# A feed-forward layer on one Trainium2 core: two x tiles are loaded later, and the order of the work on the second pair of hidden tiles is changed

## Chip, core and metric

The kernel runs on one core of one Trainium2 chip. The metric is the device time of one execution in microseconds (us). Time and profile are those of the kernel before the change, unless something else is said.

## What is computed

The input x is eight sequences of 1024 tokens by 512 channels. Cut to what matters:

```python
def cond(y, zX, zY, zR):                # a five-point stencil over tokens and channels
    lap_x = left - 2*y + right          # neighbours by reflection at the borders
    lap_y = up - 2*y + down
    return zX*lap_x + zY*lap_y + zR*y*(1 - y)

def ffn(x, W1, b1, W2, b2, scale):      # W1 is 2048 x 512, W2 is 512 x 2048
    even, odd = x[:, 1:17:2], x[:, 2:17:2]
    m1 = outer(even[:, :4], odd[:, :4])     # 2048 x 512 of rank one pieces, per sequence
    m2 = outer(even[:, 4:], odd[:, 4:])     # 512 x 2048
    h = gelu(x @ (W1 + scale*m1).T + b1)
    return h @ (W2 + scale*m2).T + b2

out = x + ffn(cond(x, zX, zY, zR), W1, b1, W2, b2, scale)
```

## The kernel before

**Work of TensorE.** All is kept transposed: y, the result of the stencil, has 128 partitions by 4 channel groups by the tokens. A sequence is 8 tiles of y (x tile n has 128 tokens with a border), two halves of 512 tokens. Layer one makes 16 hidden tiles of 128 per half in PSUM (`ph`), in 8 pairs i; layer two adds each of them into four PSUM banks `po`. Each operand is split in two fp32r parts, a high one (`yh`, `W1h`, `gh`, `W2h`: a rounded copy made by ScalarE) and a low one (`yl`, `W1l`, `gl`, `W2l`: the difference, made by VectorE), and each product is three matmuls, high by high, low by high, high by low (L629, L631, L633 for layer one in `product`, L645 to L647 for layer two in `layer2`). From sequence 1 on layer one uses Strassen's scheme. The weights W1 and W2 of each pair get the rank one piece of their sequence first: for W1, ScalarE writes `scale * outer` into a buffer (`outer`, L840), and GpSimd starts a DMA that adds W1 from HBM onto it (`add_W1`: L519 for pair 1 of sequence 0, L521 for all others); for W2, VectorE adds the piece (`fold`, L1302), whose row comes as a broadcast load.

**The first 30 us.** The change is almost all here, in sequence 0. Nothing of y exists at the start, so the first pair and the first tiles are made in ways of their own:

- PE runs 18 warm-up matmuls (L672), then makes the neighbour sums of y tile 0 (`raw0`) and tile 1 (`sums1`, from sums `st` and `sd` that VectorE forms) as matmuls by diagonals, and rows for the outer products (`even_row`).
- y tiles 0 to 3 are finished by VectorE. For tiles 0 and 1: `mul(0, n)` (L1257), then `tile0(n)` (L1219), which adds the PSUM result. For tiles 2 and 3: the two neighbour sums `sd` = up + down and `st` = left + right (for tile 2 by VectorE in `sums0(2)`, L1202 and L1203; for tile 3 by GpSimd in `sums3`, L512 and L513), then `mul`, `fin` (L1262), `tile` (L1268).
- `pair0(n)` (L610) makes hidden pair 0 from plain fp32, tile by tile of y; it waits for `s_tile`.
- Pair 1 (L639) follows as three groups of 8 matmuls: `W1h` by `yh0`, `W1l` by `yh0`, `W1h` by `yl0`. `W1h` of pair 1 is made by `w1h_plain(1)` on ScalarE (L854), which waits for `d_raw1`, the landing of L519's DMA; `W1l` by `w1l_plain(1)` on VectorE (L1252); `yh0` and `yl0` by `part0_h` (L818) and `part0_l` (L1234).
- Layer two for the first hidden tile (L700) comes next: 4 matmuls each of `gh` by `W2h`, `gl` by `W2h`, `gh` by `W2l`. `W2h` comes from `w2h(0, 0)` (L883), this from `fold(0, 0)`, and this waits for a broadcast load of rows (L361, SyncE), which itself waits until the rows were stored to HBM (L359). Then the steady order of L645 to L647 and L629 to L633 begins.

**What sets the order.** All orders are written out by hand: each engine has a list of calls, in-order, with semaphores between them. SyncE's list is that of one DMA queue (q1 in the profile), GpSimd's DMAs are another (q0), ScalarE starts the loads of x tiles 0, 2 and 3 (q10). SyncE first issues x tile 1, W1 and W2 parts, `xn`, and x tiles 4 to 7 (L244), and only then the store of the rows.

The waits that matter here are few:

```python
e.wait_ge(s_mt, 1)       # sums3: GpSimd after VectorE's second sum of tile 2
e.wait_ge(s_outer, summed(b, i))   # add_W1
e.wait_ge(d_raw1, 16)    # w1h_plain(1)
e.wait_ge(d_row2, 16)    # SyncE, between L359 and L361
```

Of the kernel before, what the change touches and what calls it, by code (L numbers as in the profile page):

```python
# [5 lines left out]
def adaln_ffn_kernel(nc: bass.Bass, xT, xs, x, xn, pk, w1, w2, b2, out):  # L6
# [3 lines left out]
    ALU = mybir.AluOpType  # L10
# [10 lines left out]
    with ctx:  # L21
# [17 lines left out]
        yh0 = sb("yh0", [128, 5, 2, 512], f32r)  # L39
        yl0 = sb("yl0", [128, 5, 2, 512], f32r)  # L40
# [194 lines left out]
        def _(e):  # L235
# [7 lines left out]
            def load_x0(n):  # L243
                e.dma_start(Xs[n].rearrange("p r s -> p (r s)"), xT[0, n]).then_inc(d_x[n], 16)  # L244
# [110 lines left out]
            e.dma_start(xr[:, 0:2, :].rearrange("p a q -> p (a q)"), xn).then_inc(d_N, 16)  # L355
            for n in (4, 5, 6, 7):
                load_x0(n)
            e.wait_ge(s_flat, 1)
# [16 lines left out]
            load_W2(0, 7)  # L375
            load_EB1(0, 5)
            load_W2(0, 8)
            keep_W1(4)
            load_W2(0, 9)
            load_EB1(0, 6)  # L380
            load_W2(0, 10)
            load_W2(0, 11)
# [119 lines left out]
        def _(e):  # L502
            def diagonal(a, v):
                return e.affine_select(DG[:, a, :], v.broadcast_to([128, 128]), [[-1, 128]],
                                       ALU.is_equal, 0.0, base=0, channel_multiplier=1)

            def sums3():
                mid, up, down, left, right = x_at(0, 3)
                st, sd = sums_at(0, 3)
                e.wait_ge(d_x[3], 16)  # L510
                e.wait_ge(s_mt, 1)
                e.tensor_tensor(sd, up, down, ALU.add).then_inc(s_md, 1)  # L512
                e.tensor_tensor(st, left, right, ALU.add).then_inc(s_mt, 1)  # L513
# [36 lines left out]
            diagonal(1, zt[:, 0, 1:2]).then_inc(s_dg, 1)  # L550
            diagonal(0, zt[:, 0, 0:1]).then_inc(s_dg, 1)
            sums3()
            for i in range(1, NI):
# [25 lines left out]
        def _(e):  # L579
# [104 lines left out]
            for bank, lt, rows in ((ph[1], 0, 2), (ph[3], 1, 3)):  # L684
                e.wait_ge(s_outer, rows)
                for s in range(2):
                    term(bank, W1h, 2 * s + lt, yh0, s, s == 0, False)
            e.wait_ge(s_w1lB, 1)
            for bank, lt in ((ph[3], 1), (ph[1], 0)):
                for s in range(2):  # L690
                    term(bank, W1l, 2 * s + lt, yh0, s, False, False)
            e.wait_ge(s_ylt, 4)
            for bank, lt, done in ((ph[3], 1, s_plain), (ph[1], 0, s_p3)):
                for s in range(2):
                    mm = term(bank, W1h, 2 * s + lt, yl0, s, False, s == 1)
                mm.then_inc(done, 1)
# [85 lines left out]
        def _(e):  # L782
# [189 lines left out]
            e.wait_ge(d_N, 16)  # L972
            e.activation(nW, nM[:, 128:384], ACT.Identity, bias=zc[:, 1, 8:9], scale=zc[:, 0, 8:9]).then_inc(s_nw, 1)
            w1h_plain(2)
            scaled(0, 4)
            w2h(0, 0)
            w2h(0, 1)

# [174 lines left out]
        def _(e):  # L1153
# [37 lines left out]
            def sums1():  # L1191
# [4 lines left out]
                e.tensor_tensor(sd, up, down, ALU.add).then_inc(s_sd1, 1)  # L1196

            def sums0(n):
                mid, up, down, left, right = x_at(0, n)
                st, sd = sums_at(0, n)  # L1200
                e.wait_ge(d_x[n], 16)
                e.tensor_tensor(sd, up, down, ALU.add).then_inc(s_md, 1)  # L1202
                e.tensor_tensor(st, left, right, ALU.add).then_inc(s_mt, 1)  # L1203
# [166 lines left out]
            mul(0, 0)  # L1370
            sums0(2)
            tile0(0)
            fold0()
            mul(0, 1)
            tile0(1)
# [7 lines left out]
            part0_l(1)  # L1383
            w1l_plain(1)
            part0_l(2)
            part0_l(3)
            glE(0, 0, 0)
            fold(0, 0, 0, 4)
# [286 lines left out]
```

## Time and profile before

| what | value |
|---|---|
| median of 3 runs | 1335.42 us (1335.19 to 1335.44) |
| the profiled execution's own time | 1335.85 us |
| its span | 1334.6 us |
| PE busy | 1330.2 us (100%), 5896 instructions |
| PE weight loads | 1099.5 us (82%) |
| VectorE, ScalarE, GpSimd busy | 1034.8, 793.3, 255.9 us |
| granted TensorE clock | 1.0 throughout |

The span is from the first to the last instruction. Matmuls overlap in the profile (each is shown with 389 ns, though the next one starts 227 ns later), so PE's busy share says only that no long gap is there; the starts of the rows tell the rest. The page's sections 2 and 4 show the same: every slice of PE is at 9 tenths or more, and the chain of work that ended last is PE for 98% of the span.

### The profile page before, as it was taken

The page shows a single profiled execution, that of the slowest core. Times are in us where ns is not written, and L with a number is a line of the kernel's source. Part 1 is how long each engine was busy: PE and PEld are TensorE (multiplying, and loading weights), DVE is VectorE, ACT ScalarE, POOL GpSimd, SP SyncE. Part 2 cuts the span into 40 slices and gives each one's busy share as a digit, 9 for nine tenths or more (in the row PEclk, how much of TensorE's full clock was granted, in tenths as well). Part 3 has the DMA queues.
Part 4 walks back from the last instruction along what each step waited for, and adds up shares of the span by engine and source line. Part 5 has one row for each costly group of instructions (what it writes and reads, how often), then busy time and mean ns, then how long its engine had stood idle before and what let it go on. Part 6 is the DMA issues. An engine that isn't in the chain of part 4 may idle for free.

```text
span 1334.6 us, 17111 instructions
## 1 busy us (share of the span) xinstructions
PE 1330.2 (100%) x5896; PEld 1099.5 (82%) x5896; DVE 1034.8 (78%) x1774; ACT 793.3 (59%) x1372; POOL 255.9 (19%) x257
## 2 busy tenths in 40 slices
PE   9999999999999999999999999999999999999999
PEld 7888888888888888888888888888888888888887
DVE  8977799858897688976899668996689967665343
ACT  6644566645675556754677546675467754666432
POOL 1000122301232012320132201331022310232000
PEclk9999999999999999999999999999999999999999
DMA  8764377777778577876768667686767866676661
GB/s 253 195 155 151 83 203 212 205 213 207 189 202 201 183 214 197 212 188 203 205 189 222 179 219 192 194 218 173 231 176 210 210 188 201 162 191 164 173 195 50
DMA packets 140224, 253.79 MB, mean 190 GB/s; under 512 B 13669, under 2 KB 37481, under 8 KB 140137
## 3 DMA queue, kind: packets, MB, share of 16 engines
q1 hardware_dynamic: 122184, 201.69, 47.1%
q0 software_dynamic: 17520, 49.81, 22.3%
q10 hardware_dynamic: 432, 1.20, 0.2%
q8 instruction: 46, 0.75, 0.2%
q14 instruction: 42, 0.34, 0.1%
HBM read 189.61 MB, written 63.05 MB: 189 GB/s over the span
## 4 chain that ended last, share of the span: by engine, by line
PE 98%; DMA 1%; ACT 1%; DVE 0%; issue 0%; SPq 0%; ACTq 0%; DVEq 0%
PE po L645 17%; PE po L646 17%; PE po L647 17%; PE ph L629 15%; PE ph L631 15%; PE ph L633 15%; DMA R<-in_w_dram 1%; DMA x<-in_xT_dram 0%; PE po L700 0%; DVE xr L1366 0%; ACT DE L944 0%; ACT y L793 0%; ACT R L840 0%; ACT UVs L840 0%; ACT W1h L854 0%
## 5 line engine op out<-in xcount | busy, mean ns | idle before, releaser
L645 PE MATMUL po<-W2h,gh 128*128 128x512 f32 x1020 | 397.1, 389 | 0.0
L647 PE MATMUL po<-W2h,gl 128*128 128x512 f32 x1020 | 397.1, 389 | 0.0
L646 PE MATMUL po<-W2l,gh 128*128 128x512 f32 x1020 | 397.0, 389 | 0.0
L629 PE MATMUL ph<-yh,W1h 128*128 128x512 f32 x896 | 348.8, 389 | 0.0
L633 PE MATMUL ph<-yh,W1l 128*128 128x512 f32 x896 | 348.8, 389 | 0.0
L631 PE MATMUL ph<-yl,W1h 128*128 128x512 f32 x896 | 348.7, 389 | 0.0
L647 PEld LDWEIGHTS po<-W2h,gl 128*128 128x128 f32 x1020 | 191.5, 188 | 39.8
L645 PEld LDWEIGHTS po<-W2h,gh 128*128 128x128 f32 x1020 | 191.5, 188 | 39.8 <-DVE W2l L1310 0.2
L646 PEld LDWEIGHTS po<-W2l,gh 128*128 128x128 f32 x1020 | 191.5, 188 | 39.6
L629 PEld LDWEIGHTS ph<-yh,W1h 128*128 128x128 f32 x896 | 168.2, 188 | 35.1 <-issue 0.2
L633 PEld LDWEIGHTS ph<-yh,W1l 128*128 128x128 f32 x896 | 168.2, 188 | 35.0
L631 PEld LDWEIGHTS ph<-yl,W1h 128*128 128x128 f32 x896 | 168.2, 188 | 34.7
L1354 DVE TENSOR_TENSOR gl<-ph,gh 128x512 fp32r<-128x512 f32 x128 | 87.8, 686 | 112.8 <-ACT gh L926 112.6
L530 POOL TENSOR_TENSOR Ts<-R 128x512 f32<-128x512 f32 x56 | 75.4, 1346 | 445.5 <-DVE W1l L1321 390.4
L1359 DVE TENSOR_TENSOR gl<-ph,gh 128x512 fp32r<-128x512 f32 x128 | 87.3, 682 | 79.7 <-ACT gh L933 79.5
L1302 DVE SCALAR_TENSOR_TENSOR W2s<-EB,SC,W2s 128x128 f32<-128x128 f32 x480 | 142.3, 346 | 3.3 <-DMA W2s<-in_w_dram 2.3
L919 ACT ACTIVATE ph<-ph,PK 128x512 f32<-128x512 f32 x128 | 84.0, 656 | 75.8 <-DVE ph L1350 71.9
L1310 DVE TENSOR_TENSOR W2l<-W2s,W2h 128x512 fp32r<-128x512 f32 x124 | 112.2, 905 | 4.3 <-ACT W2h L883 4.2
L883 ACT ACTIVATE W2h<-W2s 128x512 fp32r<-128x512 f32 x124 | 77.9, 629 | 61.7 <-DVE W2s L1302 61.1
L926 ACT ACTIVATE gh<-ph 128x512 fp32r<-128x512 f32 x128 | 76.7, 599 | 63.1 <-PE po L647 59.0
L840 ACT ACTIVATE R<-EB,SC 128x256 f32<-128x256 f32 x240 | 101.8, 497 | 0.3 <-DMA EB<-ep_scratch 0.3
L909 ACT ACTIVATE ph<-ph,PK 128x512 f32<-128x512 f32 x128 | 83.7, 654 | 29.4 <-DVE ph L1344 16.0
(125 smaller groups left out, 1365.4 us busy)
## 6 DMA issues: line engine op xcount, KB each, us to landing
W2s<-in_w_dram SPq DMA_DIRECT2D x124, 256.0 KB, 3.8
R<-in_w_dram POOLq DMA_DIRECT2D x62, 512.0 KB, 7.1
uv_scratch<-UVs SPq DMA_DIRECT2D x112, 256.0 KB, 4.4
UVs<-uv_scratch SPq DMA_DIRECT2D x112, 256.0 KB, 3.9
X<-in_xT_dram SPq DMA_DIRECT2D x56, 390.0 KB, 4.8
xr<-in_x_dram SPq DMA_DIRECT2D x16, 1024.0 KB, 5.5
xr<-in_b_dram POOLq DMA_DIRECT2D x16, 1024.0 KB, 10.6
out_dram<-xr SPq DMA_DIRECT2D x64, 256.0 KB, 2.3
```

Of the source, the lines that this page charges most:

```text
L629: e.matmul(bank[:, :], W1h[:, f, blk, wc], yh[:, q, c, :], start=first and c == 0, stop=False, skip_group_check=not first)
L631: e.matmul(bank[:, :], W1h[:, f, blk, wc], yl[:, q, c, :], start=False, stop=False, skip_group_check=not first)
L633: mm = e.matmul(bank[:, :], W1l[:, f, blk, wc], yh[:, q, c, :], start=False, stop=c == 1, skip_group_check=not first)
L645: e.matmul(po[t][:, :], gh[:, lt, st], W2h[:, k, :], start=i == 0 and lt == 0, stop=False)
L646: e.matmul(po[t][:, :], gh[:, lt, st], W2l[:, k, :], start=False, stop=False)
L647: return e.matmul(po[t][:, :], gl[:, lt, st], W2h[:, k, :], start=False, stop=i == NI - 1 and lt == 1)
L840: m = e.activation(to[:, 2 * h:2 * h + 2, 128 * c:128 * c + 128], row.rearrange("p (a q) -> p a q", a=2), ACT.Copy, scale=SC[:, b % 2, cd, ...
L919: e.activation(bank[:, :], bank[:, :], ACT.Gelu, bias=b1t[:, k:k + 1]).then_inc(s_actL, 1)
L1302: m = e.scalar_tensor_tensor(w, rows2(b, n // 4)[:, a, :], SC[:, b % 2, ck, 4 + a:5 + a], w, ALU.mult, ALU.add)
L1310: e.tensor_tensor(W2l[:, k, :], w2s_at(b, n), W2h[:, k, :].bitcast(f32), ALU.subtract).then_inc(s_w2l, 1)
L1354: e.tensor_tensor(gl[:, 0, :], bank_of(b, h, i, 0)[:, :], gh[:, 0, :].bitcast(f32), ALU.subtract).then_inc(s_glE, 1)
L1359: e.tensor_tensor(gl[:, 1, :], bank_of(b, h, i, 1)[:, :], gh[:, 1, :].bitcast(f32), ALU.subtract).then_inc(s_glL, 1)
```

## The change

Four things are done, all in the first 60 us:

1. SyncE issues the loads of x tiles 6 and 7 no longer at the start, but after the loads `load_EB1(0, 5)` and `load_EB1(0, 6)`.
2. Of tile 2's two neighbour sums VectorE keeps up + down (`side2`) and GpSimd takes left + right (`token2`), ahead of its two sums of tile 3, which no longer wait for `s_mt`. VectorE's `mul(0, 1)` moves ahead of `side2`, `tile0(0)` and `fold0`.
3. PE takes `W1h` by `yl0` of pair 1 ahead of `W1l` by `yh0`; VectorE accordingly makes the low part of y tiles 2 and 3 ahead of `W1l`.
4. ScalarE takes `w2h(0, 0)` ahead of `w1h_plain(2)` and `w2h(0, 1)` ahead of `scaled(0, 4)`.

```diff
@@ block.sync
-            for n in (4, 5, 6, 7):
-                load_x0(n)
+            load_x0(4)
+            load_x0(5)
             e.wait_ge(s_flat, 1)
             e.dma_start(R2, rows[:, :]).then_inc(d_row2, 16)
             e.wait_ge(d_row2, 16)
...
             load_EB1(0, 5)
+            load_x0(6)
             load_W2(0, 8)
             keep_W1(4)
             load_W2(0, 9)
             load_EB1(0, 6)
+            load_x0(7)
@@ block.gpsimd
+            def token2():
+                mid, up, down, left, right = x_at(0, 2)
+                e.wait_ge(d_x[2], 16)
+                e.wait_ge(s_md, 1)
+                e.tensor_tensor(sums_at(0, 2)[0], left, right, ALU.add).then_inc(s_mt, 1)
...
                 e.wait_ge(d_x[3], 16)
-                e.wait_ge(s_mt, 1)
                 e.tensor_tensor(sd, up, down, ALU.add).then_inc(s_md, 1)
                 e.tensor_tensor(st, left, right, ALU.add).then_inc(s_mt, 1)
...
+            token2()
             sums3()
@@ block.tensor
-            e.wait_ge(s_w1lB, 1)
+            e.wait_ge(s_ylt, 4)
             for bank, lt in ((ph[3], 1), (ph[1], 0)):
                 for s in range(2):
-                    term(bank, W1l, 2 * s + lt, yh0, s, False, False)
-            e.wait_ge(s_ylt, 4)
+                    term(bank, W1h, 2 * s + lt, yl0, s, False, False)
+            e.wait_ge(s_w1lB, 1)
             for bank, lt, done in ((ph[3], 1, s_plain), (ph[1], 0, s_p3)):
                 for s in range(2):
-                    mm = term(bank, W1h, 2 * s + lt, yl0, s, False, s == 1)
+                    mm = term(bank, W1l, 2 * s + lt, yh0, s, False, s == 1)
@@ block.scalar
+            w2h(0, 0)
             w1h_plain(2)
+            w2h(0, 1)
             scaled(0, 4)
-            w2h(0, 0)
-            w2h(0, 1)
@@ block.vector
+            def side2():
+                mid, up, down, left, right = x_at(0, 2)
+                e.wait_ge(d_x[2], 16)
+                e.tensor_tensor(sums_at(0, 2)[1], up, down, ALU.add).then_inc(s_md, 1)
...
             mul(0, 0)
-            sums0(2)
+            mul(0, 1)
+            side2()
             tile0(0)
             fold0()
-            mul(0, 1)
             tile0(1)
...
             part0_l(1)
-            w1l_plain(1)
             part0_l(2)
             part0_l(3)
+            w1l_plain(1)
             glE(0, 0, 0)
```

On VectorE, from the sums of tile 1 to the last tile of y, this stood in a row before (the numbers L are lines of the kernel; `s` is the buffer of neighbour sums):

```order
L1195 TENSOR_TENSOR s<-x 128x512
L1196 TENSOR_TENSOR s<-x 128x512
L1257 TENSOR_TENSOR y<-y,x 128x4x128
L1202 TENSOR_TENSOR s<-x 128x512
L1203 TENSOR_TENSOR s<-x 128x512
L1219 TENSOR_TENSOR y<-y,po 128x4x128
L1228 SCALAR_TENSOR_TENSOR UVs<-ph,SC,UVs 128x2x128 x4
L1257 TENSOR_TENSOR y<-y,x 128x4x128
L1219 TENSOR_TENSOR y<-y,po 128x4x128
L1257 TENSOR_TENSOR y<-y,x 128x4x128
L1262 SCALAR_TENSOR_TENSOR y<-s,PK,y 128x4x128
L1268 SCALAR_TENSOR_TENSOR y<-s,PK,y 128x4x128
```

and this stands there now:

```order
L1203 TENSOR_TENSOR s<-x 128x512
L1204 TENSOR_TENSOR s<-x 128x512
L1270 TENSOR_TENSOR y<-y,x 128x4x128 x2
L1209 TENSOR_TENSOR s<-x 128x512
L1232 TENSOR_TENSOR y<-y,po 128x4x128
L1241 SCALAR_TENSOR_TENSOR UVs<-ph,SC,UVs 128x2x128 x4
L1232 TENSOR_TENSOR y<-y,po 128x4x128
L1270 TENSOR_TENSOR y<-y,x 128x4x128
L1275 SCALAR_TENSOR_TENSOR y<-s,PK,y 128x4x128
L1281 SCALAR_TENSOR_TENSOR y<-s,PK,y 128x4x128
```

One sum of tile 2 is gone, and the multiplication of tile 1 stands beside that of tile 0, so that behind `fold0` (L1228, now L1241) only the addition of tile 1 is left before tile 2 is worked on.

On GpSimd, between the diagonals and the DMAs that add W1, before:

```order
L504 AFFINE_SELECT DG<-ON 128x128
L504 AFFINE_SELECT DG<-PK 128x128 x2
L512 TENSOR_TENSOR s<-x 128x512
L513 TENSOR_TENSOR s<-x 128x512
L519 DMA UVs<-in_w_dram 128x1024
L521 DMA R<-in_w_dram 128x1024 x6
```

and now:

```order
L506 AFFINE_SELECT DG<-ON 128x128
L506 AFFINE_SELECT DG<-PK 128x128 x2
L513 TENSOR_TENSOR s<-x 128x512
L519 TENSOR_TENSOR s<-x 128x512
L520 TENSOR_TENSOR s<-x 128x512
L526 DMA UVs<-in_w_dram 128x1024
L528 DMA R<-in_w_dram 128x1024 x6
```

Three sums stand ahead of the DMA of W1's pair 1 where two stood.

On SyncE, from the start of its list to the second load of x, as a difference:

```order
 L271 DMA W2s<-in_w_dram 128x512 x2
 L355 DMA xr<-in_xn_dram 128x1024
-L244 DMA x<-in_xT_dram 128x780 x4
+L244 DMA x<-in_xT_dram 128x780 x2
 L359 DMA row_scratch<-rows 4x128
 L361 DMA EB<-row_scratch 128x512
```

The store of the rows and their broadcast load stand behind two x tiles instead of four.

## Rows read from the trace of the kernel before

**Rows 1.** Timeline of PE: start us, duration us, engine, line, operation, count, and idle time before.

```profile
0.85 3.87 PE L672 MATMUL ph<-const-bfloat16-1.0 128*128 128x256 bf16 x18 [0.85 <-PEq L1665]
...
12.00 7.50 PE L610 MATMUL ph<-y,UVs 128*128 128x128 f32 x64
19.26 2.07 PE L639 MATMUL ph<-yh,W1h 128*128 128x512 f32 x8
...
22.99 1.98 PE L639 MATMUL ph<-yl,W1h 128*128 128x512 f32 x8
25.22 1.19 PE L700 MATMUL po<-W2h,gh 128*128 128x512 f32 x4 [0.26 <-ACT W2h L883]
...
28.07 0.39 PE L645 MATMUL po<-W2h,gh 128*128 128x512 f32 x1
...
1330.89 0.39 PE L647 MATMUL po<-W2h,gl 128*128 128x512 f32 x1
```

**Rows 2.** One stretch, busy us by engine: PE, PEld, DVE, ACT, POOL; clock, DMA share, GB/s.

```profile
17.00:17.50 0.50, 0.50 (x6) 0.38 (x4) 0.50 (x2) 0.07 (x1) 0.00 (x0) 1.00 1.11 197
```

**Rows 3.** Timeline of VectorE.

```profile
11.36 0.90 DVE L1257 TENSOR_TENSOR y<-y,x 128x512 f32<-128x512 f32 x1
12.36 0.69 DVE L1219 TENSOR_TENSOR y<-y,po 128x512 f32<-128x512 f32 x1
...
16.65 0.75 DVE L1268 SCALAR_TENSOR_TENSOR y<-s,PK,y 128x512 f32<-128x512 f32 x1
...
23.05 1.14 DVE L1302 SCALAR_TENSOR_TENSOR W2s<-EB,SC,W2s 128x128 f32<-128x128 f32 x4 [0.98 <-DMA EB<-row_scratch]
...
29.33 1.22 DVE L1252 TENSOR_TENSOR W1l<-R,W1h 128x1024 fp32r<-128x1024 f32 x1
```

**Rows 4.** Timeline of GpSimd.

```profile
9.43 1.28 POOL L512 TENSOR_TENSOR s<-x 128x512 f32<-128x512 f32 x1 [4.82 <-DVE s L1203]
10.67 1.03 POOL L513 TENSOR_TENSOR s<-x 128x512 f32<-128x512 f32 x1
12.00 1.03 POOL L519 DMA_DIRECT2D UVs<-in_w_dram  x1 [0.29 <-ACT UVs L840]
...
37.57 0.85 POOL L521 DMA_DIRECT2D R<-in_w_dram  x1 [21.18 <-ACT R L840]
```

**Rows 5.** Timeline of ScalarE.

```profile
17.97 1.04 ACT L854 ACTIVATE W1h<-UVs 128x1024 fp32r<-128x1024 f32 x1
...
24.55 0.61 ACT L883 ACTIVATE W2h<-W2s 128x512 fp32r<-128x512 f32 x1
...
46.82 1.05 ACT L854 ACTIVATE W1h<-R 128x1024 fp32r<-128x1024 f32 x1
...
49.69 0.80 ACT L793 ACTIVATE y<-x,zc 128x512 f32<-128x512 f32 x1
```

**Rows 6.** Timeline of SyncE's queue: the store of the rows and their broadcast load.

```profile
9.11 0.33 SPq L359 DMA_DIRECT2D row_scratch<-rows  x1
15.01 0.35 SPq L361 DMA_DIRECT2D EB<-row_scratch  x1
```

**Rows 7.** From issue to landing: L519; L521 issued at 159.6 us; L521, three issued from 37.6.

```profile
DMA to landing us min/median/max: 5.5/5.5/5.5
...
DMA to landing us min/median/max: 5.3/5.3/5.3
...
DMA to landing us min/median/max: 7.4/7.5/8.2
```

**Rows 8.** Queues, packets, MB, share of 16 engines: 9.1 to 14.7 us, then 17.4 to 21.5.

```profile
q1 hardware_dynamic: 748, 2.13, 96.3%
...
q0 software_dynamic: 134, 0.49, 63.2%
q1 hardware_dynamic: 132, 0.24, 35.1%
```

**Rows 9.** DMA issues of the first 60 us: loads of x tiles, KB, us to landing.

```profile
x<-in_xT_dram SPq DMA_DIRECT2D x5, 390.0 KB, 8.9
```

## The prediction, made before the change was run

> **What bounds the kernel now.** I read the page first: PE has work in every slice, so only gaps between matmuls can be won. The timeline of PE tells where they are. From 28.07 us to the last matmul at 1330.89 us [rows 1] there are the 5748 matmuls of the six large groups (3 x 1020 and 3 x 896 on the page), so they start (1330.89 - 28.07) / 5747 = 0.2267 us apart. Single ones are 0.227 apart wherever I looked: behind 28.07 us nothing is left to win. Whatever the change does to the time, it does by moving that first row: **the sum is the new start of the 28.07 us row, less 28.07.**
>
> Ahead of it PE has two gaps. `pair0` is 64 passes; in 17.0 to 17.5 us the weight loads are busy for 0.38 of 0.50 us and hold only 4 rows [rows 2]: PE waits for y tile 3, whose last step starts at 16.65 and ends at 17.40 us [rows 3]. Finer windows show the passes 0.107 us apart otherwise, and 64 x 0.107 = 6.9 us against 19.26 - 12.00 = 7.26 [rows 1], so this gap is about 0.35 us. The other stands ahead of L700: 25.22 - 22.99 = 2.23 us for 8 matmuls worth 8 x 0.227 = 1.82, so 0.41 us, waiting for `W2h` [rows 1]. That is made at 24.55 us [rows 5], since its `fold` waited until 23.05 us for the row broadcast [rows 3], issued only at 15.01 us because the row store of 9.11 us took so long [rows 6].
>
> Then the queues. From 9.1 to 14.7 us q1 moves 2.13 MB [rows 8], which is x tiles 4 to 7 and what stood ahead of them, and the row store lands behind them. From 17.4 to 21.5 us q0 (W1 additions) and q1 (the broadcast) move packets side by side, 134 and 132 in 4.1 us [rows 8].
>
> **Part 1: y tiles 2 and 3.** VectorE loses one sum of 0.6 us, and `mul(0, 1)` leaves the place behind `fold0` for one where VectorE has its input, as tile 1's product by ScalarE was ready. At 11.36 us the addition of tile 1 can start instead of at 12.36 [rows 3], since `sums1` is through PE by then. So y tile 3 ends at best 17.40 - 1.0 = 16.4 us and `pair0` runs without its gap: from 12.00 to 18.9 us, **0.35 us** earlier.
>
> A block between VectorE and GpSimd may take part of this. The multiplication at 11.36 us has two inputs in SBUF and took 0.90 us where its likes take 0.69, with GpSimd's sum running until 10.67 + 1.03 = 11.70 [rows 3, 4]; 11.70 + 0.6 is its end. The Trainium skill ("SBUF — State Buffer", section "SBUF: two separate sides") states that a VectorE instruction with two SBUF inputs and a GpSimd instruction that reads SBUF share a port pair by an exclusive lock, and the later one blocks fully. By that rule, the trace agrees, the multiplication of tile 2 would wait at 11.96 us for GpSimd's third sum, until about 12.7. Priced by the rows, that gives back 0.7 of the 1.0 us: y tile 3 ends at 17.1 instead of 16.4 us, and PE reaches it at about 17.2. With or without the block the gap closes, so the sum keeps 0.35 us.
>
> **Part 2: the addition of W1's pair 1.** This is what the change pays. GpSimd has three sums now: 9.43 + 1.28 + 1.03 + 1.03 gives 12.8 us, where it was free at 11.70 and issued the DMA at 12.00 us [rows 4], waiting only for ScalarE. The new issue is at 12.8 to 13.1; I take 13.0. Before, the DMA landed at 12.00 + 5.5 = 17.5 us [rows 4, 7], and the copy `W1h` ran from 17.97 to 19.01 [rows 5], just in time for PE at 19.26. Bounds for the new landing L:
> - From below: 5.3 us, that of a DMA at 159.6 us with nothing else beside it at its start [rows 7]: L = 18.3.
> - From above: 7.5 us, the middle of the three issued beside other traffic from 37.6 us on [rows 7]: L = 20.5.
> - Between: the x tiles gone from q1 are 2 x 390 KB = 0.80 MB at 2.13 MB in 5.6 us or a little more (0.41 MB/us while no other queue ran), 1.95 us. The row store then lands at 13.05 instead of 15.0 us, and the broadcast is issued there. Its first packets came 2.2 us after issue (17.2 us), so now at 15.3. The addition has 144 packets; by 15.3 us about 26 of them are through, going by the one of 159.6 us. The other 118 share the engines with the broadcast at 134 / 4.1 = 33 packets per us [rows 8]: 3.6 us, and 0.5 to the semaphore, as before: **L = 19.4 us.** So the broadcast that used to start when the addition was through now falls on it.
>
> I take 19.4, nearest to the rows of this very stage. PE then starts L639 at L + 1.04 (the copy) + 0.06 (ScalarE's end to PE, as at 25.22 us) = 20.5 us, with PE idle from 18.9. The 0.35 us of part 1 are buried under it.
>
> **Part 3: the gap ahead of L700.** The broadcast took 8.0 us (15.01 to 23.05); now it lands by 21 us. `fold(0, 0)` is behind `glE`, itself behind ScalarE's gelu, which waits for the copy `W1h`: about 22.4 us. `W2h` is made at 24.0 us, PE wants it 5.5 us after 20.5, at 26.0. **The gap of 0.41 us is gone.** Here `w2h(0, 0)` ahead of `w1h_plain(2)` costs nothing and matters only if the second W1 addition is later than now; VectorE's `W1l` of pair 2, at 29.33 + 1.22 = 30.55 us before [rows 3] for a PE start at 30.80, keeps its distance or gains.
>
> **Part 4: the PE swap.** The same 24 matmuls; `W1l` of pair 1 is wanted 1.8 us later. Made 1.2 us after `W1h`, it would have been in time for the old order too: 0, covered by the first 8 matmuls. If that cover were gone, it would cost 1.2 us at most.
>
> **Part 5: x tiles 6 and 7 later.** Each is one issue of 0.45 us and 0.40 MB on q1, at about 37.7 and 46.8 us. They land within 8.9 us [rows 9], by 46.6 and 55.7; ScalarE wants them at 49.69 [rows 5] and 59.30. Beside them run the W1 additions of pairs 4 and 5: that of 37.57 us [rows 4] lands 7.4 to 8.2 us later [rows 7], and with 1.0 us for the x tile by 46.1; its copy ran at 46.82 [rows 5]. Cost 0; without that cover W1 would be a few tenths late, and PE wants pair 4 only at 52.65.
>
> **The sum.** From the start of L639 to the 28.07 us row are 8.81 us, less the gap 0.41: 8.40. New start: 19.4 + 1.10 + 8.40 = 28.9, so **+0.8 us**. In general the change is L - 18.57. The profiled execution (1335.85) would read 1336.65; it stands 0.43 above the median of the runs, so the median comes to **1336.2 us**.
>
> **Rivals.**
> - *No collision (-0.3 us, 1335.1).* The broadcast comes later than I say or shares less, and L = 18.3. For it: the store may not gain the full 1.95 us. Against it: q1 is full without a break until the last x tile, and the store lands just behind it. At the very best (L under 17.7) PE runs gapless: -0.8 us. Chance 0.28.
> - *Full collision (+1.9 us, 1337.3).* L = 20.5, if the broadcast's packets come first or GpSimd's third sum is itself blocked by VectorE. In 17.5 to 20 us q0 got only some 22 packets per us, which speaks for it. Chance 0.17.
> - *Slower beyond measuring.* The idle time of PE ahead of L639, 1.6 to 2.7 us where the longest now is 0.4, slows the matmuls after it. The warm-up matmuls of 256 columns started 3.87 / 18 = 0.215 us apart [rows 1], later ones of 512 columns 0.227, so PE has a pace of half per column at the start. A stretch as long as the warm-up at half pace costs 1.9 us; on top of the full collision that makes +3.8, 1339.2 us. It decides from the point where the gap is long enough to lose the pace; no row has one. The Trainium skill ("TensorE: Matmul & The Clock Gate", section "Part 1: The HAM clock gate") says the array falls back to 1.2 GHz once it has been idle long enough. The granted clock reads 1.00 in every window before, around the 0.4 us gap too. Chance 0.04.
> - *The change does not do what it says:* the x tiles' cost comes back later, at 37 to 60 us, as a W1 copy that is late for PE. Part 5's distances of 0.7 us and more speak against it, the queues' crowding there for it: +0.5 to +1.5 us, 0.03, within the range.
>
> **The numbers.** The forecast has 0.48. Measurement tells apart about 0.2%, 2.7 us; the best case gains 0.8 us, so faster gets 0.01; same gets 0.95 and slower 0.04. The range holds the forecast, both collisions' bounds and the gapless case with some tenths for the runs: 1334.5 to 1337.8.
>
> **What would show it.** Right: VectorE's tile-1 addition at about 11.4 us; GpSimd's DMA at about 13.0; the broadcast issued at about 13.1; `W1h` of pair 1 at 19.4; PE idle some 1.6 us ahead of L639; no gap at L700; the first steady matmul at 28.9. Wrong: W1's landing before 18.5 us, or a broadcast issued only at 15 us. If W1 lands by 18.5 and the time is still longer, my claim that nothing behind 28.07 us can move is what failed.

## The result, and the profile after

| | before | changed |
|---|---|---|
| median | 1335.44 us (1335.19 to 1336.73, 7 runs) | **1340.34 us** (1338.99 to 1341.27, 7 runs) |
| profiled execution, its span | 1335.85, 1334.6 us | 1340.26, 1339.0 us |
| first steady matmul | 28.07 us [rows 1] | 32.71 us |

The changed kernel is slower: the ratio is 1.0034 (1.0024 to 1.0044), 4.9 us by the medians. The prediction said 1336.2 us, 0.8 more than before, and no more than 1337.8. It was wrong; in direction and place it was right, in size it was out by a factor of six.

The timeline of PE in the changed kernel, with the same columns as [rows 1]:

```profile
12.56 7.31 PE L618 MATMUL ph<-y,UVs 128*128 128x128 f32 x64
22.96 3.52 PE L647 MATMUL ph<-yh,W1h 128*128 128x512 f32 x8 [3.09 <-issue]
26.31 2.02 PE L647 MATMUL ph<-yl,W1h 128*128 128x512 f32 x8
28.17 1.98 PE L647 MATMUL ph<-yh,W1l 128*128 128x512 f32 x8
29.99 1.07 PE L708 MATMUL po<-W2h,gh 128*128 128x512 f32 x4
...
32.71 0.39 PE L653 MATMUL po<-W2h,gh 128*128 128x512 f32 x1
...
1335.36 0.39 PE L655 MATMUL po<-W2h,gl 128*128 128x512 f32 x1
```

Everything lies ahead of 32.71 us: behind it the same 5748 matmuls start (1335.36 - 32.71) / 5747 = 0.2267 us apart, as before. So the new start of that row is the place to look. It is 4.64 us later, and the rows share this out:

- `pair0` starts 0.56 us later (12.56 for 12.00).
- From there to pair 1 (now L647) it takes 10.40 us where it took 7.26: +3.14. PE stands idle for 3.09 us in the middle of it.
- The 24 matmuls of pair 1 and what stood between them and L708 take 7.03 us for 5.96: +1.07. Before, 0.41 of the 5.96 was the gap for `W2h`, so the matmuls themselves took 5.55, and now 1.48 more.
- The 12 matmuls of L708 take 2.72 us for 2.85: -0.13.

0.56 + 3.14 + 1.07 - 0.13 = 4.64 us.

The first item is no cost of the change: over the thirteen traces `pair0` starts anywhere between 11.96 and 13.01 us, with the change in both of these, and here PE waits for `W1h` in any case. The two first items together, 3.70 us, are how much later pair 1 starts.

ScalarE's timeline tells what PE waited for:

```profile
21.80 1.06 ACT L862 ACTIVATE W1h<-UVs 128x1024 fp32r<-128x1024 f32 x1 [3.93 <-DMA UVs<-in_w_dram]
...
25.84 0.63 ACT L891 ACTIVATE W2h<-W2s 128x512 fp32r<-128x512 f32 x1
...
49.81 1.05 ACT L862 ACTIVATE W1h<-R 128x1024 fp32r<-128x1024 f32 x1
```

The copy `W1h` of pair 1 ran at 17.97 us before [rows 5]. Now ScalarE waits 3.93 us for the W1 addition and starts at 21.80. The addition was issued here, on GpSimd:

```profile
9.38 1.04 POOL L513 TENSOR_TENSOR s<-x 128x512 f32<-128x512 f32 x1 [4.84 <-DVE s L1209]
10.39 1.27 POOL L519 TENSOR_TENSOR s<-x 128x512 f32<-128x512 f32 x1
11.62 1.03 POOL L520 TENSOR_TENSOR s<-x 128x512 f32<-128x512 f32 x1
12.60 1.01 POOL L526 DMA_DIRECT2D UVs<-in_w_dram  x1
```

and SyncE issued the row store and its broadcast load here:

```profile
9.06 0.32 SPq L359 DMA_DIRECT2D row_scratch<-rows  x1
13.20 0.36 SPq L361 DMA_DIRECT2D EB<-row_scratch  x1
```

So the addition is issued only 0.6 us later than before [rows 4], and even a little earlier than forecast. But it takes 9.2 us to land where it took 5.5 [rows 7]; the broadcast takes 5.0 for 8.0. From issue to landing, L526 and then L361:

```profile
DMA to landing us min/median/max: 9.2/9.2/9.2
...
DMA to landing us min/median/max: 5.0/5.0/5.0
```

The packets by queue (q0 GpSimd's, q1 SyncE's; packets, MB, share of 16 engines), first in 14.1 to 16.7 us, then in 17.7 to 21.3 us:

```profile
q1 hardware_dynamic: 85, 0.17, 40.6%
...
q0 software_dynamic: 198, 0.75, 104.8%
q1 hardware_dynamic: 2, 0.00, 0.2%
```

Between 12.7 and 14.0 us both queues show one packet together. Then the broadcast runs alone for 2.6 us, on 40.6% of the engines' time, while the addition issued 0.6 us ahead of it has not moved a packet. Its first ones come at about 16.8 us, 4.2 us after its issue; from then on q0 is full.

The last 1.5 us are the clock. Stretches of 1 us of the changed kernel, with the columns of [rows 2]:

```profile
22.00:23.00 1.00, 0.04 (x1) 0.07 (x1) 0.11 (x1) 1.00 (x2) 0.00 (x0) 0.83 1.08 213
23.00:24.00 1.00, 1.00 (x3) 0.81 (x4) 1.00 (x1) 0.97 (x3) 0.00 (x0) 0.50 1.01 201
24.00:25.00 1.00, 1.00 (x4) 0.81 (x3) 1.00 (x4) 0.97 (x3) 0.00 (x0) 0.50 0.93 240
25.00:26.00 1.00, 1.00 (x4) 0.79 (x3) 1.00 (x5) 0.87 (x3) 0.00 (x0) 0.50 0.95 350
26.00:27.00 1.00, 1.00 (x5) 0.75 (x4) 1.00 (x4) 1.00 (x2) 0.00 (x0) 0.96 0.17 64
```

The granted clock goes from 1.00 to 0.50 (2.4 to 1.2 GHz) between 22 and 23 us, while PE is idle, and comes back at about 26.0. The first 8 matmuls of pair 1 take 26.31 - 22.96 = 3.35 us for 1.9.

### The profile page after: what moved, and what is told of

Its sections match the earlier page's. It is cut to its first block, busy times and chain, and to the rows that moved or that the text cites. A ratio compares the mean times of both kernels' runs of the same rounds, so it can differ in the third digit from the quotient of the medians.

```text
span 1339.0 us, 17111 instructions
## 1 busy us (share of the span) xinstructions
PE 1331.8 (99%) x5896; PEld 1100.6 (82%) x5896; DVE 1036.6 (77%) x1773; ACT 794.5 (59%) x1372; POOL 257.2 (19%) x258
## 3 DMA queue, kind: packets, MB, share of 16 engines
q0 software_dynamic: 17520, 49.81, 22.0%
## 4 chain that ended last, share of the span: by engine, by line
PE 99%; issue 0%; DVE 0%; DVEq 0%
PE po L654 17%; PE po L655 17%; PE po L653 17%; PE ph L637 15%; PE ph L639 15%; PE ph L641 15%; PE ph L647 1%; PE ph L618 1%; PE ph L680 0%; PE po L593 0%; PE po L708 0%; DVE xr L1379 0%; PE ph L611 0%; PE po L598 0%; PE po L603 0%
```

## The experiments

The first theory (A in the expectations) was that the **earlier broadcast holds the W1 addition back**, and that the idle time it makes brings the clock down. The rivals: the addition is late because it is issued 0.6 us later, behind a third sum; the new orders of PE, VectorE or ScalarE cost the time; the clock has no part in it. Each batch of kernels had its own runs of the kernel before, whose medians were 1335.78 (the first four runs below), 1335.87 (the next four) and 1335.89 us (the last three). Ratios and differences from the kernel before are against those of the same batch. The changed kernel was not run again in them; a difference from its 1340.34 us sets two batches side by side, whose kernels before lie 0.3 to 0.5 us apart. Edits are against the changed kernel, except in the two runs that start from the kernel before.

### Only the x tiles later

```diff
-            for n in (4, 5, 6, 7):
-                load_x0(n)
+            load_x0(4)
+            load_x0(5)
...
+            load_x0(6)
...
+            load_x0(7)
```

(in the kernel before; the rest is as it was)

> The kernel before with one part of the change alone: x tiles 6 and 7 loaded after the pieces of pairs 5 and 6. GpSimd then issues W1's addition for pair 1 at 12.0 us as before, and the row broadcast is issued at about 13.1 us. Theory A (a broadcast that gets its packets going first holds back the start of the addition): the addition lands at 20.5 us or later, TensorE idles 2 us or more ahead of L639, and the time is 2 us or more above before. Theory B (the addition starts late because of GpSimd's own third sum and a block by VectorE, whatever the broadcast does): it lands at 17.5 to 18.5 us and the time is within 0.5 us of before, or up to 0.4 us under it, since the gap ahead of L700 closes. Theory of the prediction (both share packet by packet from 15.3 us): landing at 18.3 us, no gain or loss over 0.5 us.

Measured: 1336.20 us (1335.52 to 1340.54, 10 runs), ratio 1.0009 (1.0000 to 1.0019). The traced run took 1335.81 us, and in it the addition landed in 5.6 us. In it the broadcast is as early as in the changed kernel, but the addition was issued 1.08 us ahead of it. GpSimd's row, SyncE's, and the queues from 13.6 to 16.6 us:

```profile
11.99 1.03 POOL L521 DMA_DIRECT2D UVs<-in_w_dram  x1 [0.27 <-ACT UVs L842]
...
13.07 0.35 SPq L361 DMA_DIRECT2D EB<-row_scratch  x1
...
q0 software_dynamic: 118, 0.48, 105.1%
```

This time q1 is the one without a packet: the broadcast is held back to about 16.7 us. So theory A as stated, an early broadcast is enough, fell in most runs. Eight of the ten took 1335.5 to 1337.9, the other two 1340.51 and 1340.54, the changed kernel's time. What was left was a theory of **order**: one of the two transfers goes first, the other waits for nearly all of it, and which goes first hangs on a few tenths of a microsecond. The two long runs have no trace; that the broadcast went first in them is inferred from their time.

### The changed kernel with its x tiles at the start again

```diff
-            load_x0(4)
-            load_x0(5)
+            for n in (4, 5, 6, 7):
+                load_x0(n)
```

(and the two later loads taken out)

> The changed kernel with x tiles 6 and 7 loaded at the start again; all else of the change stays. The broadcast is then issued at 15 us, the addition at 12.6 to 13.0 us. Theory A: the addition lands 5.5 us after issue, at 18.1 to 18.5 us, W1h of pair 1 is there at 19.2 to 19.6 us, the clock stays at 1.00 and the time is 1335.0 to 1335.8 us. Theory B: the addition lands after 20.5 us, and the time stays 3 us or more above before.

Measured: 1335.89 us (1335.66 to 1336.62, 10 runs), ratio 0.9999 (0.9990 to 1.0009). The addition is issued at 12.61 us, as late as in the changed kernel, and `W1h` is copied at 18.06, with PE running from `pair0` on without a gap. The broadcast is issued at 15.28. The later issue of the addition, the rival, costs nothing by itself.

### The broadcast held until the addition has landed

```diff
+            e.wait_ge(d_raw1, 16)
             e.dma_start(EB2[:, :, :], ...)    # L361
```

> The changed kernel, but SyncE issues the row broadcast only after W1's addition for pair 1 has landed. Theory A: the addition lands at 12.6 + 5.3 to 5.5 = 18.0 us, TensorE starts L639 at 19.2 us, the broadcast lands at 23 to 24 us, late for L700 by up to 1 us; time within 0.7 us of before either way. Theory B: the addition lands at 21.8 us as in the change, and the broadcast even later, 26 us: 5 us or more above before.

Measured: 1338.61 us (1337.93 to 1339.46), ratio 1.0020 (1.0011 to 1.0030). The landing came as expected; the time did not, at 2.8 us above before instead of within 0.7. Rows of ScalarE, SyncE, VectorE and PE:

```profile
18.17 1.06 ACT L863 ACTIVATE W1h<-UVs 128x1024 fp32r<-128x1024 f32 x1 [0.54 <-DMA UVs<-in_w_dram]
...
18.23 0.35 SPq L362 DMA_DIRECT2D EB<-row_scratch  x1
...
25.24 1.14 DVE L1316 SCALAR_TENSOR_TENSOR W2s<-EB,SC,W2s 128x128 f32<-128x128 f32 x4 [4.11 <-DMA EB<-row_scratch]
...
27.10 1.67 PE L709 MATMUL po<-W2h,gh 128*128 128x512 f32 x4 [2.07 <-ACT W2h L892]
```

The addition, issued at 12.61, lands by 18.2: 5.5 us, with nothing else changed but the broadcast. That is the collision shown from its other side. The new cost is the mirror image: the broadcast, issued at 18.23, meets additions 2 and 3 in q0, and the queues from 18.3 to 21.5 us show q0 alone:

```profile
q0 software_dynamic: 174, 0.65, 103.4%
```

VectorE gets the rows at 25.24 us, PE waits 2.07 us for `W2h`, and the clock falls here too: 0.80 in 27 to 28 us, 0.50 from 28 to 31. The 12 matmuls of L709 take 31.54 - 27.10 = 4.44 us for 2.72. These two, the longer wait and the clock, are what the expectation lacked.

### PE kept at work while it waits

```diff
+            for _ in range(16):
+                e.matmul(po[0][:, 0:256], one[0], one[1], start=True, stop=True)
```

(between `pair0` and pair 1)

> The changed kernel with 16 matmuls of ones more (bf16, 256 columns, into a PSUM bank that is free) between pair 0 and L639, about 1.7 us of TensorE's idle 3.3 us. The addition still lands at 21.8 us. If the fall of the granted clock to 0.50 behind the idle time costs what the rows say (8 matmuls in 3.35 us instead of 1.9), the clock stays at 1.00 and the time is 1.5 us under the change, 3.4 us above before. If the clock's fall hides behind other waits, the time is that of the change.

Measured: 1338.96 us (1338.64 to 1340.64, 10 runs), ratio 1.0024 (1.0015 to 1.0033). PE's rows of pair 1 and of layer two:

```profile
22.80 2.09 PE L647 MATMUL ph<-yh,W1h 128*128 128x512 f32 x8 [0.69 <-issue]
24.73 1.99 PE L647 MATMUL ph<-yl,W1h 128*128 128x512 f32 x8
...
28.37 1.07 PE L710 MATMUL po<-W2h,gh 128*128 128x512 f32 x4
```

The addition lands as late as ever (`W1h` at 21.65), PE starts pair 1 at the same time, and the 24 matmuls take 5.57 us instead of 7.03, the clock at 1.00. The rows give 7.03 - 5.57 = 1.46 us. By the medians the kernel gains 1340.34 - 1338.96 = **1.4 us**, or 4.90 - 3.18 = 1.7 us if each is first taken against the kernel before of its own batch. So the clock's share of the 4.9 us is 1.4 to 1.7, and the rest, 3.2 to 3.5, is the late landing's. One of the ten runs took 1340.64 at a lower mean clock, so the filling does not always hold.

### The broadcast one microsecond later

```diff
+            e.wait_ge(s_outer, 2)
             e.dma_start(EB2[:, :, :], ...)    # L361
```

> The changed kernel with one wait more: SyncE issues the row broadcast only when ScalarE has written the outer product of pair 2, at about 14.4 us instead of 13.2 us. Order theory (which of the two transfers gets its first packet out first keeps the other back; the addition needs 1.4 us from issue to packet, the broadcast 0.8): the addition of 12.6 us goes first at 14.0 us and lands at 18.1 us; the broadcast lands at 20 to 21 us; TensorE has no gap of over 0.2 us, the clock stays at 1.00; the time is 4.5 us under the change and 0 to 0.8 us under before. Rival (crowding as such delays the addition, however the order): it lands at 19.5 us or later and the time is 1 us or more above before.

Measured: 1335.67 us (1335.39 to 1336.26, 11 runs), ratio 0.9999 (0.9990 to 1.0007). Rows of GpSimd, SyncE, ScalarE and PE:

```profile
12.83 1.01 POOL L527 DMA_DIRECT2D UVs<-in_w_dram  x1
...
14.25 0.35 SPq L362 DMA_DIRECT2D EB<-row_scratch  x1
...
18.34 1.06 ACT L863 ACTIVATE W1h<-UVs 128x1024 fp32r<-128x1024 f32 x1 [0.49 <-DMA UVs<-in_w_dram]
...
12.39 7.31 PE L619 MATMUL ph<-y,UVs 128*128 128x128 f32 x64
19.49 2.06 PE L648 MATMUL ph<-yh,W1h 128*128 128x512 f32 x8
```

This is the plainest run. Everything of the change is in it, the x tiles later too; the broadcast alone is issued at 14.25 us instead of 13.20, and the median is 4.7 us lower. The addition lands in 5.5 us, pair 1 starts 7.10 us after `pair0`, and no gap is left from there to the end. The expectation's 1.4 us from the addition's issue to its first packet was too short: it is 14.5 - 12.83 = 1.7 us here.

### The addition ahead of GpSimd's last sum

```diff
+                add_W1(0, 1)        # between the two sums of tile 3
...
-            for i in range(1, NI):
+            for i in range(2, NI):
```

> The changed kernel, with GpSimd issuing W1's addition for pair 1 between its two sums of tile 3, at 12.0 us instead of 12.6 us; the broadcast is issued at 13.2 us as in the change. Order theory: the distance from issue to issue is 1.2 us instead of 0.6, the addition goes first and lands at 17.5 us in most runs; time 0 to 0.8 us under before, with a few runs near 1340 us where the broadcast wins, as in the run with the x tiles late alone. The last sum of tile 3 ends at about 14.1 us, ahead of its use at 15.4 us. Rival: 0.6 us of lead changes nothing, the time stays near 1340 us.

Measured: 1336.45 us (1335.42 to 1337.91, 11 runs), ratio 1.0004 (0.9995 to 1.0013). GpSimd's rows:

```profile
12.20 1.03 POOL L527 DMA_DIRECT2D UVs<-in_w_dram  x1 [0.53 <-ACT UVs L849]
12.95 1.36 POOL L521 TENSOR_TENSOR s<-x 128x512 f32<-128x512 f32 x1
```

The broadcast is issued at 13.11, 0.91 us behind the addition, which lands in 6.2 us. No run came near 1340. The order is turned, but the time is 0.6 us above before where 0 to 0.8 under it was expected: `pair0` takes 8.00 us instead of 7.31, since y tile 3 ends at 18.62 us instead of 16.96. A row of VectorE tells why:

```profile
12.64 2.23 DVE L1271 TENSOR_TENSOR y<-y,x 128x512 f32<-128x512 f32 x1
```

The last sum itself ends at 12.95 + 1.36 = 14.31 us, well ahead of the steps of tile 3 that begin at 16.36. But the multiplication of tile 2, which does not use it, takes 2.23 us beside it where 0.69 is usual, and ends at 14.87, 0.56 us behind it. All of VectorE's work on tiles 2 and 3 is late by that.

This run also shows that the waiting has an exception. The broadcast's first packets come at about 15.5 us, when 64 of the addition's 144 are through, and from 15.8 to 17.6 us both queues run side by side:

```profile
q0 software_dynamic: 67, 0.26, 73.2%
q1 hardware_dynamic: 68, 0.14, 26.1%
```

Hence the 6.2 us for 5.5.

The same with the x tiles at the start again:

> As the run with the addition between the sums of tile 3, but x tiles 6 and 7 are loaded at the start, so that the broadcast is issued at 15 us. The addition lands at 17.5 us in every run, none near 1340 us. The broadcast lands at 20 to 23 us, so that a gap of up to 0.4 us ahead of L700 may stay: time 0 to 0.5 us under before.

Measured: 1335.84 us (1335.52 to 1337.03), ratio 1.0001 (0.9992 to 1.0010). Addition at 12.09, broadcast at 15.12, landing 5.5 us; `pair0` 7.63 us. Here VectorE's step behind that multiplication (L1274) is the slow one, 1.93 us for 0.75, again ending 0.56 us behind GpSimd's sum.

And with the wait of the run before it (`wait_ge(s_outer, 2)`) as well:

> Both together on the changed kernel: the addition issued at 12.0 us between the sums of tile 3, and the broadcast only when the outer product of pair 2 is written, at about 14.2 us. Order theory: the addition always goes first, lands at 17.5 us, the broadcast at 20 us, no run near 1340 us, TensorE without a gap from 12 us on: 0.4 to 0.9 us under before, the best of all versions. Rival: the gain in TensorE's gaps does not show in the time, within 0.2 us of before.

Measured: 1336.64 us (1335.59 to 1337.14), ratio 1.0004 (0.9995 to 1.0013). The landing is as short as can be had (5.4 us), but `pair0` takes 8.00 us again, with the same 2.23 us for the multiplication of tile 2 (12.68 to 14.91, GpSimd's sum to 14.35). I had expected the best of all; I had left out that the sum I pushed back holds up VectorE while it runs, as the prediction had said of the sum in its old place.

### A plain load in the broadcast's place

```diff
-            e.dma_start(EB2[:, :, :], bass.AP(R2.tensor, 0, [[0, 128], [128, 4], [1, 128]])).then_inc(d_f0, 16)
+            e.dma_start(EB2[:, :, :].rearrange("p a q -> p (a q)"), w2[1]).then_inc(d_f0, 16)
```

> The changed kernel, with the row broadcast (one row of 2 KB to 128 partitions in pieces of 512 B) replaced by a plain load of the same 256 KB, 2 KB to each partition, at the same place in SyncE's queue; the rows are then those of a piece of W2, so what is folded into W2 for the first four tiles is not the product it should be. Broadcast theory (the addition is held back for as long as the broadcast's packets run, and they run 3.6 us because of their form): the plain load is through in about 0.7 us, the addition's first packets come at about 14.7 us and it lands by 19 us; time 3.5 us or more under the change. Rival (any transfer that gets ahead holds the addition back by a fixed amount, or it is late by itself): it lands at 21 us or later, time as the change.

Measured: 1336.46 us (1335.86 to 1336.69, 10 runs), ratio 1.0003 (0.9994 to 1.0012). The load is issued at 13.12 us, 0.51 behind the addition (12.61), and goes first, as the broadcast does. The queues from 14.0 to 14.9 us, then from 15.6 to 18.5:

```profile
q1 hardware_dynamic: 68, 0.14, 68.7%
...
q0 software_dynamic: 157, 0.58, 107.7%
q1 hardware_dynamic: 11, 0.01, 0.7%
```

The same 256 KB land in 3.0 us instead of 5.0, and the addition comes 2.9 us sooner (`W1h` at 18.86 for 21.80). The addition's first packets come at 15.3 us here and at 16.8 in the changed kernel, so it is held back longer by a transfer that runs longer, and not by a fixed time. The broadcast runs longer because its packets go slowly, 85 in 2.6 us against the plain load's 68 in 0.9. Whether that is the pieces of 512 bytes or the source, one row of 2 KB read 128 times, this run does not tell, since it changes both.

### Only x tile 7 later

```diff
+            load_x0(6)          # at the start
...
-            load_x0(6)
```

> The changed kernel with x tile 6 loaded at the start again, so that only tile 7 is late. The row store then lands about 1.0 us later, and the broadcast is issued at 14.1 to 14.2 us, 1.5 us behind the addition. Order theory: the addition goes first and lands at 18.1 us; time 1335.3 to 1336.0, 4.5 us under the change. If instead each 0.4 MB taken from the start costs its share, the time lies halfway, at 1338.

Measured: 1335.73 us (1335.45 to 1336.28, 10 runs), ratio 0.9998 (0.9989 to 1.0007). The broadcast is issued at 14.38 us, 1.51 behind the addition, which lands in 5.7, at 18.6 us. One tile of 0.40 MB ahead in q1 is enough to keep the order.

### Only the orders

The kernel before with PE's swap and the new orders of VectorE and ScalarE; GpSimd's third sum and the x tiles as before.

```diff
-            e.wait_ge(s_w1lB, 1)
+            e.wait_ge(s_ylt, 4)
...
-                    term(bank, W1l, 2 * s + lt, yh0, s, False, False)
+                    term(bank, W1h, 2 * s + lt, yl0, s, False, False)
```

(and the lists of `w1h_plain(2)`, `scaled(0, 4)`, `w1l_plain(1)`)

> The kernel before with the orders of the second pair alone (TensorE's swap of the low terms, VectorE's low part of W1 behind that of y, ScalarE's W2 copies ahead); loads and GpSimd as before. Both theories: no difference, within 0.3 us of before, since the gap ahead of y tile 3 and the one ahead of L700 stay as they are.

Measured: 1335.87 us (1335.59 to 1336.26), ratio 1.0000 (0.9991 to 1.0009). The orders cost nothing. The gaps did not stay as expected, though: in the trace `pair0` runs through in 7.31 us, having started at 12.89, so late that y tile 3 (17.96 us) was in time, and L700 follows without a wait, `W2h` being made at 23.18 us, ahead of pair 2's `W1h`.

### What the runs say together

Issue times from the timelines of GpSimd and SyncE, landing of the addition, medians, and their difference from the kernel before of the same batch:

| kernel | addition, broadcast issued | apart | addition lands in | median us | against before |
|---|---|---|---|---|---|
| plain load for the broadcast | 12.61, 13.12 | 0.51 | 6.2 us | 1336.46 | +0.57 |
| changed | 12.60, 13.20 | 0.60 | 9.2 | 1340.34 | +4.90 |
| PE kept at work | 12.49, 13.15 | 0.66 | 9.1 | 1338.96 | +3.18 |
| addition first | 12.20, 13.11 | 0.91 | 6.2 | 1336.45 | +0.58 |
| x late only | 11.99, 13.07 | 1.08 | 5.6 | 1336.20, two of ten at 1340.5 | +0.42 |
| broadcast 1 us later | 12.83, 14.25 | 1.42 | 5.5 | 1335.67 | -0.20 |
| one tile late | 12.87, 14.38 | 1.51 | 5.7 | 1335.73 | -0.16 |
| addition first, broadcast later | 12.24, 14.62 | 2.38 | 5.4 | 1336.64 | +0.77 |
| x at start | 12.61, 15.28 | 2.67 | 5.4 | 1335.89 | +0.11 |
| orders alone | 12.37, 15.29 | 2.92 | 5.6 | 1335.87 | -0.02 |
| before | 12.00, 15.01 | 3.01 | 5.5 | 1335.44 | |
| addition first, x at start | 12.09, 15.12 | 3.03 | 5.5 | 1335.84 | -0.03 |
| broadcast held | 12.61, 18.23 | 5.62 | 5.5 | 1338.61 | +2.83 |

The later addition alone (x at start) costs nothing. The earlier broadcast alone (x late only) costs nothing in most runs and the full price in two of ten. The later addition (+0.6 us) and the earlier broadcast (-1.8 us) together shrink a distance of 3.0 us to 0.6, and there the order turns over.

The rows also say where it should turn. Where nothing else moves, the addition's first packets come about 1.7 us after its issue in the six traces that show it, those of the broadcast or the plain load 0.9 to 1.0 us in three. So the second transfer gets ahead if it is issued less than some 0.7 to 0.8 us behind the addition: at 0.51, 0.60 and 0.66 us it did, at 0.91 and more it did not in any trace.

No version beats the kernel before: the two best, 0.20 and 0.16 us under the median of their batch, have intervals that take in 1.

## Why the prediction was wrong, point by point

**Part 2 failed, at two sentences. The first:** "Its first packets came 2.2 us after issue (17.2 us), so now at 15.3." I took the 2.2 us for the broadcast's own delay. It was not: in the kernel before the queues from 14.8 to 17.0 us show

```profile
q0 software_dynamic: 120, 0.45, 103.6%
```

and not one packet of q1, though the broadcast had been issued at 15.01. It was being held back by the addition then. Its own delay is 14.1 - 13.20 = 0.9 us, seen in the changed kernel, where nothing is ahead of it; the addition's is about 1.7 (first packets at 14.4 in the third run above, 13.7 in the first, 14.5 in the fifth). The row that would have told this was in the trace of before.

**The second weighs more:** "The other 118 share the engines with the broadcast at 134 / 4.1 = 33 packets per us". With the right start of the broadcast but this sharing, all 144 packets of the addition would have gone from 14.3 us on at 33 per us, and the landing would still have come at about 14.3 + 4.4 + 0.5 = 19.2 us (an estimate from the same rows). What the trace shows instead is no sharing at all until 16.8 us, and the landing at 21.8. I read the queues from 17.4 us on only [rows 8], where q0 and q1 do share, 134 and 132 packets. That is what the second W1 addition, queued behind the first, and the broadcast do once both are running, and I carried it over to how a transfer starts beside another one.

The Trainium skill ("DMA: Bandwidth & Descriptors", section "Queues, rings and completion order") says that each DMA engine takes turns between the queues it has work for, packet by packet. The 17.4 to 21.5 us stretch of the kernel before agrees; the 2.6 us of the changed kernel in which q1 moved packets at 40.6% and q0 none do not, unless the engines had no work of q0 yet.

**The sum.** The formula of the prediction was L - 18.57. With the true landing of 21.8 us in place of 19.4 it gives +3.2 us. The upper bound, 20.5 from the 7.5 us row [rows 7], was too low: I used the middle of three additions issued beside other traffic, while the 62 issues of that line in the trace of before go further:

```profile
DMA to landing us min/median/max: 5.3/7.1/9.8
```

With 9.8 us the range would have reached L = 13.0 + 9.8 = 22.8.

**The clock** makes up the rest. The rival "slower beyond measuring" had the mechanism: idle PE ahead of pair 1, then a stretch at half pace. It put +1.9 us on it; the rows show 1.48, and the run that kept PE at work gained 1.4 to 1.7. Together with the landing the rival said 1339.2 us, 1.1 below the result. Its chance of 0.04 was a second error, and it hung on that of Part 2: it needed an idle time near its upper end, which my wrong L made unlikely. That PE falls back to 1.2 GHz after idling is what the Trainium skill ("TensorE: Matmul & The Clock Gate", section "Part 1: The HAM clock gate") says, and the trace agrees.

**Part 1 held.** VectorE's rows of the changed kernel:

```profile
11.87 0.69 DVE L1232 TENSOR_TENSOR y<-y,po 128x512 f32<-128x512 f32 x1
12.48 0.73 DVE L1270 TENSOR_TENSOR y<-y,x 128x512 f32<-128x512 f32 x1
...
16.21 0.75 DVE L1281 SCALAR_TENSOR_TENSOR y<-s,PK,y 128x512 f32<-128x512 f32 x1
...
22.89 1.23 DVE L1265 TENSOR_TENSOR W1l<-UVs,W1h 128x1024 fp32r<-128x1024 f32 x1 [3.52 <-ACT W1h L862]
```

y tile 3 ends at 16.96 us, between the 16.4 and 17.1 of the text, and `pair0` has no gap: 7.31 us for 7.50. The tile-1 addition came at 11.87, not 11.4, since PE was through with `sums1` only at 11.83; in the run with the broadcast held, where PE was through at 11.23, it came at 11.32. The block between VectorE and GpSimd is there as the prediction described it. The multiplication of tile 2 took only 0.73 us, but because it started at 12.48, just ahead of the end of GpSimd's third sum at 12.65; it ended 0.56 us behind that sum. Where it started earlier it took 1.12 to 1.30 us (four traces with the sum in this place), and ended 0.54 to 0.56 us behind the sum in each. GpSimd's second sum was not slowed: it took 1.27 us, as the same sum did before ([rows 4], 1.28).

**Part 3 held:** no wait stands ahead of L708, `W2h` being ready at 26.5 us for a start at 29.99 (that late start helped; in the run with the later broadcast there is no gap either, at 25.02). Its reason was not complete. In the run with the x tiles late alone the rows were there at 22.00 us instead of 23.05, and PE still had a gap of 25.31 - 23.02 - 1.82 = 0.47 us, because `W2h` stood behind pair 2's `W1h` and was made at 24.64. So `w2h(0, 0)` ahead of `w1h_plain(2)` does matter: the earlier broadcast alone leaves the gap. **Part 4 held:** the orders alone cost nothing. **Part 5 held:** the x tiles are issued at 39.90 and 50.20 us, the `W1h` copies near them run with distance (that of 49.81 us waits for nothing), and behind 32.71 us the spacing is that of before. That nothing behind the first steady matmul can move was right as well.

**What stays open.** In the two best kernels both of PE's gaps are gone, 0.35 + 0.41 us (one of the two has a new one of 0.21 ahead of pair 1), and only some 0.2 us show. Over the traces `pair0` starts anywhere from 11.96 to 13.01 us, mostly since the first 6 matmuls of `raw0` take 2.74 to 3.66 us; the traced run of the kernel before was an early one. Later waits on VectorE, GpSimd or a DMA may absorb a late start in the kernel before and not where the gaps are gone. The trace with the orders alone shows this once for the gap in `pair0`; it was not tried by itself. Also open is what holds the second transfer back: whether the engines, the queues or the making of their descriptors. The runs tell only that it happens, in both directions, and how long.

## What to carry to other kernels

When a change moves two transfers on different queues to within about a microsecond of each other, ask which gets its first packet out, and price the other as waiting for most of it; a transfer's time to its first packet can't be read from a row where another was ahead of it. Work taken off a queue lets what stands behind it come sooner, and that can be the wrong thing: here a broadcast that was wanted only some microseconds later got ahead of the addition that PE was waiting for. Where the wait so made leaves PE idle for a few microseconds, add the clock to it. And an instruction moved on GpSimd can hold up VectorE while it runs, even one whose result VectorE does not need yet.

## What the hardware showed unexpectedly

- **A transfer can wait for most of one on another queue that started first, even if that one leaves the engines more than half idle.** The addition's first packets came 4.2 us after its issue instead of 1.7, behind a broadcast at 40.6% of the engines' time that was some 60% through by then; the broadcast in its turn was held by additions, to 2.2 us after its issue before and to some 3.6 us after it when issued at 18.23, instead of 0.9. It is no firm rule: with 0.91 us between the issues the broadcast began when 44% of the addition was through. What decides this is open.
- **The tip lies between 0.66 and 0.91 us between issues** in the traces, the addition being issued first. By the times of ten runs of one kernel, it went both ways where the traced run had 1.08 us; the distance in the two long runs is not known.
- **VectorE's multiplication of two SBUF operands waited for GpSimd's sum to end.** In the seven traces of the changed kernel and its variants where the multiplication of tile 2 overlaps the third sum, it ended 0.54 to 0.56 us behind the end of the sum, whether that made it 0.73 or 2.23 us long. In the two where it did not start before that end (12.66 and 12.93 us) it took 0.69 and 0.68 us.
- **The clock fell behind an idle time of 2.07 us, after PE had started again.** In the run with the held broadcast it read 1.00 in 26 to 27 us, while PE stood still, 0.80 in 27 to 28 and 0.50 in the next three stretches; PE had started at 27.10, and the fall came at about 27.6. The stretches from 26 to 29 us:

```profile
26.00:27.00 1.00, 0.00 (x0) 0.00 (x0) 1.00 (x4) 0.59 (x2) 0.00 (x0) 1.00 0.01 2
27.00:28.00 1.00, 0.90 (x3) 0.77 (x4) 1.00 (x5) 0.99 (x2) 0.00 (x0) 0.80 0.00 0
28.00:29.00 1.00, 1.00 (x4) 0.71 (x4) 0.90 (x3) 0.94 (x2) 0.00 (x0) 0.50 0.00 0
```

  The price, 4.44 - 2.72 = 1.7 us, was no smaller than behind the 3.1 us of the changed kernel. A gap of 0.69 us left it at 1.00.
